# Attention scores written to four PSUM banks of a phase instead of two in turn

## What is computed

```python
q = (x @ w_q + b_q).reshape(B, Lq, 16, 32)        # x already layer-normalised
k = (context @ w_k + b_k).reshape(B, -1, 16, 32)
v = (context @ w_v + b_v).reshape(B, -1, 16, 32)
scores = einsum('bqhd,bkhd->bhqk', q, k) / sqrt(32)
weights = softmax(scores, axis=-1)
out = einsum('bhqk,bkhd->bqhd', weights, v).reshape(B, Lq, D) @ w_o + b_o
```

## Time and profile before

| | us |
|---|---|
| median of 3 runs | 1703.21 (1697.96 to 1706.17) |
| the profiled execution, its own time | 1706.38 |
| its span, first to last instruction | 1704.5 |
| mean granted TensorE clock, share of full speed | 0.971 |
| busy over the span: PE, DVE, ACT, POOL | 1528.9, 1190.5, 1121.4, 1022.1 |

### The profile page before, as it was taken

One profiled execution on the slowest core, in us unless ns is written; L12 is line 12 of the kernel. 1 busy time (PEld: TensorE's weight loads), 2 busy tenths in 40 slices (PEclk: granted clock), 3 DMA queues, 4 the chain that ended last, 5 costly groups with the idle time before them and its releaser, 6 DMA issues. The chain is left out here.

```text
span 1704.5 us, 28818 instructions
## 1 busy us (share of the span) xinstructions
PE 1528.9 (90%) x8836; PEld 671.3 (39%) x8836; DVE 1190.5 (70%) x1438; ACT 1121.4 (66%) x1895; POOL 1022.1 (60%) x738
## 2 busy tenths in 40 slices
PE   5999878998999974899999999999999968999998
PEld 3545433443444431333333334343433313444443
DVE  4978898997989755666676767676676646655552
ACT  5667598887888743566666666666666656566662
POOL 4767437766778722566666666666666664554442
PEclk9989899999999996999999999999999988999999
DMA  8411000000000112121211112111211100010001
GB/s 310 147 64 46 1 1 1 1 1 1 0 1 1 46 51 80 32 57 34 53 34 46 47 33 54 32 54 33 56 37 35 53 30 25 25 49 25 25 25 50
DMA packets 61226, 72.18 MB, mean 42 GB/s; under 512 B 15312, under 2 KB 40784, under 8 KB 60624
## 3 DMA queue, kind: packets, MB, share of 16 engines
q1 hardware_dynamic: 57968, 62.36, 12.4%
q10 hardware_dynamic: 3168, 8.78, 1.3%
HBM read 37.40 MB, written 8.39 MB: 27 GB/s over the span
## 5 line engine op out<-in xcount | busy, mean ns | idle before, releaser
L1594 DVE TENSOR_REDUCE s_mx<-bank 128x2 f32<-128x1024 f32 x256 | 301.6, 1221 | 207.4 <-PE bank L1719 207.4
L1471 ACT ACTIVATE s_E<-bank 128x512 f32<-128x512 f32 x512 | 281.6, 596 | 204.2 <-PE bank L1735 198.0
L1355 POOL TENSOR_TENSOR s_E<-s_E 128x1024 f32<-128x1024 f32 x128 | 302.5, 2375 | 92.5 <-ACT s_E L1471 92.5
L1735 PE MATMUL bank<-s_QA,s_KA 97*128 97x512 f16 x512 | 179.3, 389 | 28.0 <-DMA s_QA<-s_mrow 7.5
L1908 POOL TENSOR_TENSOR sm_cx<-m_xf,sm_cx 128x512 f16<-128x512 f32 x60 | 84.1, 1407 | 104.5 <-ACT sm_cx L1950 104.5
L1743 PE MATMUL bank<-s_E,s_V 128*32 128x512 f32 x1024 | 139.0, 615 | 4.6 <-ACT s_E L1471 2.8
L1076 PE MATMUL bank<-sm_zz,w1raw 128*128 128x512 f16 x256 | 99.3, 388 | 28.7 <-DVE sm_cx L963 15.5
L1598 DVE RECIPROCAL bank<-bank 128x256 f32<-128x256 f32 (+1 forms) x66 | 112.7, 1708 | 17.2 <-PE bank L1751 17.2
L1099 PE MATMUL bank<-f_w2q,w2raw 128*128 128x512 f16 x512 | 121.8, 379 | 0.6 <-DVE w2raw L951 0.3
L773 POOL TENSOR_TENSOR sm_wkv<-sm_wkv,sm_cx 128x511 f32<-128x511 f32 x48 | 66.1, 1377 | 90.1 <-DVE sm_wkv L963 80.6
L767 POOL TENSOR_TENSOR w1raw<-w1raw,sm_cx 128x512 f32<-128x512 f32 x88 | 115.6, 1334 | 2.3 <-ACT sm_cx L855 2.3
(11 more groups left out here) (268 smaller groups left out, 4038.2 us busy)
## 6 DMA issues: line engine op xcount, KB each, us to landing
sm_cx<-in_ctx SPq DMA_DIRECT2D x16, 768.0 KB, 4.5
X<-in_x SPq DMA_DIRECT2D x8, 1024.0 KB, 6.8
s_QA<-sm_cx SPq DMA_DIRECT2D x256, 32.0 KB, 1.9
out_x<-X SPq DMA_DIRECT2D x8, 1024.0 KB, 4.3
s_KA<-sm_cx SPq DMA_DIRECT2D x244, 32.0 KB, 1.9
w1raw<-in_w ACTq DMA_DIRECT2D x1, 4096.0 KB, 14.2
w2raw<-in_w ACTq DMA_DIRECT2D x1, 4096.0 KB, 27.9
s_QA<-s_qkh SPq DMA_DIRECT2D x128, 32.0 KB, 1.8
```

What stands on the lines that cost most here:

```text
L1355: e.tensor_tensor(into, into, other, ALU.add).then_inc(s_sum.sem, 1)
L1471: e.activation(E[:, SLOT[k] + h, :], SC[u % 2][:, :], ACT.Exp, scale=1.0 / float(np.sqrt(DH)))\
L1594: e.tensor_reduce(mx[:, 2 * i:2 * i + 2, q], MAXED[i][:, :, :], AX.X, ALU.max).then_inc(s_red.sem, 1)
L1735: e.matmul(SC[u % 2][:, :], KA[0:MROW + 1, m, h, t * P:(t + 1) * P], QA[0:MROW + 1, m, h, :], start=True, stop=True).then_inc(s_sc.sem, 1)
```

## The change

A phase's four scores go to the four banks that its maxima have used: score h to bank h. Scores 0 and 1 are issued after reduction i = 0, scores 2 and 3 after reduction i = 1, and the wait for exponential u - 2 is dropped, since all four banks were already empty of exponentials when the maxima were issued. Where there is no next group (the last step), everything is as before. `rows` moves from bank 2 to bank 0 and gets a wait for the exponential of unit 12 of the step before, which read bank 0. The two places of the last output tiles that take over banks 2 and 3 wait accordingly. No arithmetic, DMA or tile shape changes.

```diff
-        SC, MX, MAXED, NUM, DEN, R6, R7 = banks[0:2], banks[0:4], pairs[0:2], banks[4], banks[5], banks[6], banks[7]
+        MX, MAXED, NUM, DEN, R6, R7 = banks[0:4], pairs[0:2], banks[4], banks[5], banks[6], banks[7]
+        s_bank = lambda u, nxt: MX[u % (4 if nxt else 2)]
...
-            def exponential(b, m, u):
+            def exponential(b, m, u, nxt):
...
-                e.activation(E[:, SLOT[k] + h, :], SC[u % 2][:, :], ACT.Exp, scale=1.0 / float(np.sqrt(DH)))\
+                e.activation(E[:, SLOT[k] + h, :], s_bank(u, nxt)[:, :], ACT.Exp, scale=1.0 / float(np.sqrt(DH)))\
...
-                e.activation(mrow[:, :], MX[2][0:4 * TT, 0:P], ACT.Copy, scale=-1.0 / MS).then_inc(s_mrow.sem, 1)
+                e.activation(mrow[:, :], MX[0][0:4 * TT, 0:P], ACT.Copy, scale=-1.0 / MS).then_inc(s_mrow.sem, 1)
...
             def rows(b, m):
+                s_ex.wait(e, b, 16 * m - 3)
                 e.wait_ge(s_red.sem, s_red.count(b, 2 * TT * (m + 1)))
-                e.transpose(MX[2][0:4 * TT, 0:P], mx[:, :, :].rearrange("p h q -> p (h q)"), ident[:, :]).then_inc(s_mT.sem, 1)
+                e.transpose(MX[0][0:4 * TT, 0:P], mx[:, :, :].rearrange("p h q -> p (h q)"), ident[:, :]).then_inc(s_mT.sem, 1)
...
-                if nxt and h == 0:
-                    e.wait_ge(s_red.sem, s_red.count(nxt[0], 2 * (TT * nxt[1] + t) + 1))
-                s_ex.wait(e, b, 16 * m + u - 1)
-                e.matmul(SC[u % 2][:, :], KA[0:MROW + 1, m, h, t * P:(t + 1) * P], QA[0:MROW + 1, m, h, :],
+                if nxt and h % 2 == 0:
+                    e.wait_ge(s_red.sem, s_red.count(nxt[0], 2 * (TT * nxt[1] + t) + h // 2 + 1))
+                if not nxt:
+                    s_ex.wait(e, b, 16 * m + u - 1)
+                e.matmul(s_bank(u, nxt)[:, :], KA[0:MROW + 1, m, h, t * P:(t + 1) * P], QA[0:MROW + 1, m, h, :],
...
                 if c == 0:
-                    if i == 2:
-                        s_mrow.wait(e, b, NG)
-                    elif i == 3:
+                    if i < 4:
                         e.wait_ge(s_red.sem, s_red.count(b, 2 * TT * NG))
+                        e.wait_ge(s_ex.sem, s_ex.count(b, 16 * (NG - 1)))
```

More of the change, by code:

```diff
@@ L1530, in step @@
                 for u in range(UNITS):
-                    exponential(b, m, u)
+                    exponential(b, m, u, nxt)
                     if m == 1 and u in T_AT:
@@ L1563, in _ @@
             for m in range(2):
-                values(0, m, SC[m])
+                values(0, m, MX[m])
             queries(0, 1, 0, R6)
```

## The result

The changed kernel takes 1675.13 us (median of 4 runs, 1673.91 to 1676.41) against 1704.69 for the kernel before in the same session (4 runs, 1697.96 to 1707.64): a ratio of 0.9832, interval 0.9801 to 0.9863, 29.6 us less. The forecast was 1681.6, or 21.6 less, in a range of 1670 to 1697.

The account below looks back on a forecast made before the run. PE's own queue was taken to close phases like (0,0), exponentials some others. Six middle batches gave 17.6 us, first and last 2 x 2.0, in sum 21.6 us: 1681.6 us against the median of 1703.2, range 1670 to 1697.

Parts of the forecast that it names:

- What bounds the stage: Attention: neither VectorE's reductions nor ScalarE's exponentials bound it; PE's own queue closes phase (0,0), exponentials close phase 2.
- Score 2 and score 3: Phase (0,0): loaded at 0.88 and 1.10 after the first score, products at 1.32, maxima at 2.92; phase gains 0.32.
- The zero phases: Phases (1,2), (1,3), (2,2), hanging on unmoved ScalarE and VectorE work, and (2,0), (3,0), where no score waits: gain 0.
- The sum: Gain over the 16 phases of a middle batch: 1.60 + 0.70 + 0.49 + 0.15 = 2.94 us per batch.
- (0,3): Phase closed by the transposed maxima, whose chain stands behind score 3 on PE: gain about 0.39 us.
- First and last batch: Fewer products and no next group at the end: two thirds of a middle batch's gain each, 2 x 2.0 us.
- What may absorb it: ScalarE's 0.33 us idle ahead of phase (1,2) just fits PE arriving 0.32 earlier; VectorE has 0.14 left.
- A: Rival: gain given back, only the exponentials' own advance stays, about 0.9 us per batch, 7 in all: 1696 us; chance 0.10.
- B: Rival: `mrow` and its DMA decide where (0,3) and (3,3) end; 5.6 us less gain, 1687 us; chance 0.06.
- C: Rival: score bursts and longer pauses drop PE's clock to 1.2 GHz, costing 40 us: 1722 us; chance 0.04.
- D: Rival: second reduction released as late as exponential 0 in most phases, so little gained: 1703 to 1699 us; chance 0.04.
- The last sign of being wrong: In any phase, a first score coming later than 2.2 us after its maxima would show the prediction wrong.

Follow-up runs that it names:

- e2: Changed kernel with score 2 waiting for exponential 0 again, score 3 still free; 1688.4 us, ratio 0.9896 to the kernel before, batch period 89.30 us.
- e7: Changed kernel with score 3 waiting for exponential 1 again, score 2 still free; 1702.84 us, ratio 0.9998 to the kernel before, batch period 91.53 us.
- e4: Changed kernel with four banks only in the nine phases PE's queue closes, two banks and old waits in the other seven; 1679.35 us, ratio 0.9851, period 88.59.
- e5: Changed kernel with four banks only in the seven phases PE's queue does not close, old scheme in the other nine; 1701.9 us, ratio 1.0002, period 91.45.
- e3: Changed kernel with one more, always met wait at score 0 of each phase; 1678.49 us, ratio 0.9841 to the kernel before, batch period 88.34 us.
- e6: Changed kernel with one more, always met wait at score 2 of each phase; 1678.36 us in a single run, batch period 88.49 us.
- e1: Changed kernel with the old waits for exponentials put back, scores still in four banks; 1706.52 us, ratio 1.0003 to the kernel before, batch period 91.69 us.
- e8: Changed kernel with each phase's maxima issued in two pairs, the first after exponentials 0 and 1; 1674.37 us, ratio 0.9846, period 88.71 against 88.27.

## Why the prediction was right, point by point

- **What bounds the stage**: PE's own queue between the waits, with exponentials closing some phases. Right: e2 against e7, and e4 against e5.
- **Score 2 and score 3**: right to 0.01 us in phase (0,0), and the 0.32 that it gains. The same pattern in (1,0), (1,1) and (2,1) put the maxima at 2.92 as worked out. In (0,1) they moved from 3.12 to 2.77; they follow the last of its small products by 0.20 in both kernels (950.17 and 950.37 before, 934.20 and 934.40 after), so the queue closes this phase too.
- **The zero phases**: right in the sum. From first score to first score, (1,2) takes 7.00 us in both kernels and (2,2) 5.94. Up to the maxima (1,2) grew by 0.07, to 4.90 (956.74 to 961.64) from 4.83 (974.16 to 978.99), and (2,2) by as much. The prediction named growth of these phases as a sign of being wrong; here it only means that the first score, now 0.05 instead of 0.12 behind its reduction, starts 0.07 earlier while VectorE's work behind it does not move. PE waits longer for it:

```profile
956.74 0.29 PEld L1738 LDWEIGHTS bank<-s_QA,s_KA 97*128 97x128 f16 x2
...
959.75 0.42 PEld L151 LDWEIGHTS bank<-ident,s_z 128*128 128x128 f32 x4 [1.77 <-DVE sm_zz L1588]
961.64 0.10 PEld L1720 LDWEIGHTS bank<-sm_cx 32*128 32x128 f16 x4 [0.42 <-issue]
```

- **The sum**: too small, 2.94 us per batch where 3.55 were measured in batch 3. The gain of each phase, from its first score to that of the next, before less after:

| phases | forecast | measured |
|---|---|---|
| (0,0), (0,1), (1,0), (1,1), (2,1) | 1.60 | 1.92 |
| (0,3) | 0.39 | 0.55 |
| (3,3) | 0.31 | 0.30 |
| (3,1), (3,2) | 0.49 | 0.59 |
| (2,3) | 0.14 | 0.02 |
| (0,2) | 0.01 | 0.08 |
| (1,2), (1,3), (2,0), (2,2), (3,0) | 0 | 0.08 |
| sum, before rounding | 2.94 | 3.55 |

  Two terms were mis-sized. The prediction set the fewer waits of the sequencer against the new one and called both nothing. In the first row 0.21 of the missing 0.32 is the first score of (0,2), (1,2) and (2,2), each 0.07 sooner behind its reduction; part of that is lost again in the phase that follows. As a whole, one idle wait is worth 0.07 us per batch at score 0 (e3) and about 0.2 at score 2 (e6), and the 0.13 that e1 keeps goes with the release of the maxima, which shrank from 0.12 to 0.05. If the three add, which no run tests, they are about 0.4 of the missing 0.61. The other term is (0,3), taken as 0.39:

```profile
941.25 0.15 PEld L1738 LDWEIGHTS bank<-s_QA,s_KA 97*128 97x128 f16 x2
...
944.13 0.27 ACT L1490 ACTIVATE s_mrow<-bank 16x128 f16<-16x128 f32 x1 [0.27 <-PE bank L1726]
...
944.71 0.13 PEld L1720 LDWEIGHTS bank<-sm_cx 32*128 32x128 f16 x4 [0.46 <-issue]
```

  The first score to the maxima takes 3.46 there, against 4.01 (957.38 to 961.39) before, so 0.55: score 3 moved by more than taken, from 1.69 to 0.99 after the first score. The maxima still follow `mrow` closely, by 0.58 (0.63 in the earlier trace rows). A miss the other way: (2,3) gained 0.02 and not 0.14, since its scores 0 and 2 hang on the reductions (score 2 goes 0.05 behind the second one).
- **First and last batch**: 26.8 us in all less 21.2 for batches 1 to 6 (551.36 us from the first score of batch 1 to that of batch 7 before, 530.15 after) leaves 5.6, where 4.0 was a guess by proportion: 3.3 in the first batch (91.94 to 88.67) and 2.3 in the last.
- **What may absorb it**: nothing did at phase (1,2); the gain of (1,1) passed ScalarE.
- **The rivals**: A would have left a period above 91, it is 88.27. B: the heads of the steps gave way with the queue, 0.55 in (0,3) and 0.30 in (3,3). C: the clock reads 1.00 as before; the rule of the Trainium skill, TensorE: Matmul & The Clock Gate, section "A second HAM failure mode: psum-queue depth-cycling", describes a loss that does not appear in this kernel, with scores as well as maxima going round four banks. D: the second reduction was ready in time in phase (0,0), and where it was not, score 2 went 0.05 behind it; that took a wait of 0.16 to 0.20 in five phases, not 0.2 or more in most. The last sign of being wrong, a first score more than 2.2 us after its maxima, could not decide: the first score of (0,3) came 2.29 us after its maxima in the kernel before already, and no such stretch grew.
- **The miss of 8 us** between 21.6 and the measured 29.6: 5.2 are the change's, since the attention gave 26.8 in the profiled pair (3.6 from the six middle batches, 1.6 from the first and last). The other 2.8 lie outside the attention or in the spread of four runs each; against the 21 later runs of the kernel before (median 1703.07) the changed kernel's median is 27.9 less.

## What to carry to other kernels

A removed wait is worth what the last instruction behind it in the same queue gains before the next point that everything has to pass; so look for the last of several waits for the same producer and take them away together, since the first alone mostly hands its idle time to the next (e7). Where other work is queued behind the waiting instruction, its start is the gain, not the start of the instruction itself. A spare buffer that is provably free already, here two banks just emptied by another stage's reader, is a cheap way to drop such a wait; where the engine's own queue is the bound, starting its consumers earlier brought nothing (e8).

## What the runs showed of the hardware that was not expected

- A second semaphore wait ahead of a matmul's weight load costs 0.07 us when it comes behind the one that matters, though it is met already (e3, e6). In the changed kernel a load held by a reduction comes 0.05 us after the reduction's end; with the idle wait it comes 0.12 after it, as in the kernel before.
- Stages whose code is the same in two kernels can differ by some us in one execution and keep the difference: the last matmul of one line (L601) ahead of the attention started at 194.6 us before, 189.4 after, and between 188.4 and 192.9 in the eight experiments. What makes the difference is not shown. A gain of 1 or 2% is read more surely from a period inside the changed stage than from the end of the program.
